# Attention scores from two rounded 4-byte parts in the two row halves of the array, in one ring of three double buffers

## What is computed

```python
x = x + layernorm(attention(layernorm(x)))      # 16 heads of size 8, rotary positions, causal softmax
x = x + layernorm(ffn(layernorm(x)))            # 16 experts, top 2, and 2 shared experts

q, k, v = split(h @ Wq + bq), split(h @ Wk + bk), split(h @ Wv + bv)
q, k = apply_rope(q, cos, sin), apply_rope(k, cos, sin)
att = einsum('bhqd,bhkd->bhqk', q, k) / sqrt(8)
att = softmax(where(causal, att, -1e10))
y = einsum('bhqk,bhkd->bhqd', att, v).reshape(B, T, 128) @ Wp + bp
```

## Time and profile before

| | |
|---|---|
| median of 3 runs | 1123.39 us (1121.81 to 1124.06) |
| the profiled execution | 1124.22 us |
| its span on the core | 1122.3 us |
| mean granted TensorE clock | 0.964 |
| PE busy | 1048.8 us (93%) |
| DVE busy | 835.8 us (74%) |
| POOL busy | 826.6 us (74%) |
| ACT busy | 745.5 us (66%) |

### The profile page before, as it was taken

The page is one execution under the profiler, slowest core; times in us unless marked ns, Lnnn a source line. Parts: engine busy times, 40 slices in busy tenths (PEclk is TensorE's granted clock), DMA queues, the critical chain, the costliest instruction groups (busy, mean ns, idle before and its releaser), DMA issues.

```text
span 1122.3 us, 26491 instructions
## 1 busy us (share of the span) xinstructions
PE 1048.8 (93%) x8228; PEld 668.9 (60%) x8228; DVE 835.8 (74%) x2265; ACT 745.5 (66%) x1619; POOL 826.6 (74%) x976
## 2 busy tenths in 40 slices
PE   3379999999999999999999999999977999999996
PEld 2255555656666566565665656656453787877742
DVE  5378888888788878888888887887255777777644
ACT  5117778787787877778777787787823666666434
POOL 6536678788888978888788886666844766666757
PEclk8559999999999999999999999999988999999998
DMA  6333333414243242432424323241556444554376
GB/s 95 110 105 119 93 94 113 116 63 121 87 139 113 63 120 73 148 109 74 122 64 140 111 79 112 73 127 38 133 156 106 137 136 137 154 155 134 109 250 199
DMA packets 109747, 129.88 MB, mean 116 GB/s; under 512 B 17723, under 2 KB 90412, under 8 KB 105004
## 3 DMA queue, kind: packets, MB, share of 16 engines
q1 hardware_dynamic: 100908, 110.04, 35.0%
q0 software_dynamic: 8704, 18.17, 4.8%
HBM read 80.99 MB, written 45.50 MB: 113 GB/s over the span
## 4 chain that ended last, share of the span: by engine, by line
PE 77%; DVE 9%; issue 2%; POOL 1%; DMA 1%; ACT 1%; SPq 0%; POOLq 0%; DVEq 0%; ACTq 0%
PE heads_ps L1535 13%; PE score L1525 10%; PE wide L1677 8%; DVE mx L1324 7%; PE wide L1499 6%; PE wide L1564 6%; PE score L1511 4%; PE wide L1566 4%; PE wide L1660 3%; PE wide L1661 3%; PE score L1651 3%; PE wide L1598 2%; PE misc L1543 2%; PE wide L1590 1%; PE wide L1618 1%
## 5 line engine op out<-in xcount | busy, mean ns | idle before, releaser
L978 ACT ACTIVATE values<-score 128x512 f32<-128x512 f32 (+1 forms) x704 | 369.0, 558 | 90.7 <-PE score L1525 81.0
L1324 DVE TENSOR_REDUCE mx<-wide 128x2 f32<-128x1024 f32 (+3 forms) x384 | 387.5, 1039 | 48.5 <-PE wide L1566 45.6
L1525 PE MATMUL score<-qk 75*128 75x512 bf16 (+3 forms) x1024 | 229.8, 301 | 1.7 <-ACT values L978 0.9
L890 POOL TENSOR_SCALAR_AFFINE_SELECT values<-values 128x512 f32<-128x512 f32 x256 | 162.1, 644 | 88.2 <-ACT values L978 87.9
L935 POOL DMA_INDIRECT token_scratch<-spread,e_id x144 | 137.9, 957 | 71.0 <-issue 52.9
L1564 PE MATMUL wide<-qk 72*128 72x384 bf16 (+2 forms) x768 | 168.3, 279 | 9.9 <-DVE mx L1324 4.9
L1535 PE MATMUL heads_ps<-values 128*32 128x512 f32 (+3 forms) x2048 | 174.3, 441 | 0.2 <-POOL values L890 0.2
L1566 PE MATMUL wide<-qk 118*128 118x128 bf16 x1024 | 170.8, 222 | 2.4 <-DVE mx L1324 1.5
L879 POOL DMA_INDIRECT sorted_scratch<-zr,places x128 | 134.0, 1047 | 48.9 <-issue 27.4
L1525 PEld LDWEIGHTS score<-qk 75*128 75x128 bf16 x1024 | 84.8, 98 | 89.8 <-ACT values L978 46.8
L1564 PEld LDWEIGHTS wide<-qk 72*128 72x128 bf16 x768 | 76.0, 99 | 65.5 <-DVE mx L1324 19.0
(11 more groups left out here) (192 smaller groups left out, 1991.3 us busy)
## 6 DMA issues: line engine op xcount, KB each, us to landing
qk<-parts_scratch SPq DMA_DIRECT2D x192, 192.0 KB
parts_scratch<-spread SPq DMA_DIRECT2D x16, 768.0 KB, 8.3
qk<-sorted_scratch SPq DMA_DIRECT2D x144, 66.5 KB
front<-token_scratch SPq DMA_DIRECT2D x16, 512.0 KB, 4.8
xt<-attn_x SPq DMA_DIRECT2D x16, 256.0 KB, 8.6
xr<-attn_x SPq DMA_DIRECT2D x16, 256.0 KB, 8.8
x_scratch<-z SPq DMA_DIRECT2D x16, 256.0 KB, 6.2
shared_scratch<-s_out SPq DMA_DIRECT2D x16, 256.0 KB, 8.8
```

The source lines that it names most:

```text
L890: nc.gpsimd.affine_select(out=prob[n][:, :, 0:P], in_=prob[n][:, :, 0:P], compare_op=ALU.is_ge, fill=0.0, base=0, pattern=[[0, HG], [1, P] ...
L978: nc.scalar.activation(free_ap(prob[kb][:, hs_[0], :], [[1, N * len(hs_)]]), score[SCORE_RING.buffer(b, step)][:, 0:N * len(hs_)], ACT.Exp ...
L1324: nc.vector.tensor_reduce(mx[:, h0:h0 + len(hs_), j:j + 1], src, axis=AX.X, op=ALU.max).then_inc(p1_max, 1)
L1525: last = nc.tensor.matmul(score[SCORE_RING.buffer(b, step)][:, k * N:(k + 1) * N], k4[e][0:SROWS, h, kb * P:(kb + 1) * P], q4[e][0:SROWS, ...
```

## The change

- **Parts.** Queries and keys are split into two parts of a rounded 4-byte type (`F32R`) in place of three bf16 parts: ACT writes the first, DVE the second; the steps `second` and `third` go. Four products of parts make 32 rows, with two maximum rows 34 (`SROWS`), with the staircase (five entries in a row) 60 (`MROWS`).
- **Row halves.** Head h lies in partitions 0 to 63 and head h + 8 in 64 to 127 of the same column block. Each matmul of p and s is issued once for each half, into the two banks of one buffer. The number of score matmuls of a batch stays: 64 in s, 112 in p.
- **Units.** s has 6 units for a group in place of 11; an exponential reads both banks. p keeps 24 units for a batch.
- **Ring.** One ring of three buffers of two banks for p, s, D and the rest (60 uses in a pass); the ring of `score` goes.
- **Heads.** The value blocks of even groups stand in columns 0 to 8, of odd groups in 9 to 17, and two groups accumulate in the same PSUM bank: two copies, two sets of four transposes and two reciprocals for a batch in place of four; the products on DVE stay four; the copy of V becomes two.
- **Maxima.** Two parts: step O and one ACT operation go; four DMAs for half the heads in place of three.
- **DMA.** Parts to DRAM 1024 KB for a batch (768 before); 20 shuffle transfers for a batch in place of 14.
- **Start.** The staircase is spread by two ACT copies and eight DMAs from the ACT queue, in place of two ACT and two DVE copies and two DMAs.
- **Order.** `START`, `ORDER` and `DRAIN` are new.

```diff
-P1_UNITS = [(3, (0, 1)), (3, (2, 3)), (2, (0, 1)), (2, (2, 3)), (1, (0, 1, 2, 3)), (0, (0, 1, 2, 3))]
-P2_UNITS = ([(0, (h,)) for h in range(HG)] + [(1, (h,)) for h in range(HG)]
-            + [(2, (0, 1)), (2, (2, 3))] + [(3, (0, 1, 2, 3))])
+P1_UNITS = [(3, (0,)), (3, (1,)), (2, (0,)), (2, (1,)), (1, (0, 1)), (0, (0, 1))]
+P2_UNITS = [(0, (0,)), (0, (1,)), (1, (0,)), (1, (1,)), (2, (0, 1)), (3, (0, 1))]
...
+    "v3.1@-1 mask2.1 p18@0 s0.0 rnormal v3.2@-1 p19@0 v3.3@-1 s0.1 p20@0 heads1@-1 s0.2 p21@0 s0.3 p22@0 K place Y "
+    "rstd s0.4 p23@0 v0.0 s0.5 cos s1.0 W p0 M1@0 mask2.2 N1@0 normal zstats s1.1 mask2.3 v0.1 s1.2 mask3.0 p1 U1 G1 "
+    "d3 v0.2 p2 s1.3 v0.3 p3 s1.4 H2 mask3.1 d4 p4 v1.0 p5 s1.5 p6 s2.0 p7 mask3.2 v1.1 s2.1 d5 p8 sin0@4 v1.2 "
+    "mask3.3 v1.3 H0@-1 d6 p9 mask0.0@1 s2.2 sin1@4 U2 d7 V rstats G2 mask0.1@1 sin2@4 p10 s2.3 sin3@4 stats d0@-1 "
+    "s2.4 d1@-1 mask0.2@1 heads0 mask0.3@1 p11 s2.5 d2@-1 T v2.0 s3.0 p12 v2.1 s3.1 mask1.0@1 zrstd@0 p13 rX v2.2 "
+    "mask1.1@1 M0 Z@0 p14 s3.2 rL choose N0 mask1.2@1 X@4 s3.3 p15 v2.3 mask1.3@1 residual@0 v3.0 chosen rexp s3.4 "
+    "p16 R@4 U0@-1 G0@-1 D mask2.0@1 Q@4 H1@-1 s3.5 rrstd@0 p17 "
...
-WIDE_STEPS = ("V", "X", "Q", "Y", "W", "T", "p", "rX", "rL", "U")
+WIDE_STEPS = ("V", "X", "Q", "Y", "W", "T", "p", "rX", "rL", "U", "s", "D", "rows")
-    WIDE_RING = Ring(B, lambda step: int(step.what in WIDE_STEPS), 2)
-    SCORE_RING = Ring(B, lambda step: SCORE_STEPS.get(step.what, 0), 2)
+    WIDE_RING = Ring(B, lambda step: int(step.what in WIDE_STEPS), 3)
...
+            for n in range(2):
+                nc.scalar.activation(qkr[0:HALF_ROWS, n, 0, :], free_ap(stairs[:, n, :], [[0, NT], [1, P]]), ACT.Copy).then_inc(stairs_set, 1)
+            act.wait_ge(stairs_set, 2)
+            for e in range(2):
+                for side in range(2):
+                    first = 0 if e or side else 1
+                    for n in range(2):
+                        act.dma_start(words[side * HALF_ROWS + ROWS:(side + 1) * HALF_ROWS, 2 * e + n, first:NH // 2, :],
+                                      free_ap(words[ROWS:HALF_ROWS, n, 0, :], [[0, NH // 2 - first], [1, T]])).then_inc(rows_filled, 16)
...
-                        for k, h4 in enumerate(hs_):
-                            h = g * HG + h4
-                            last = nc.tensor.matmul(score[SCORE_RING.buffer(b, step)][:, k * N:(k + 1) * N],
-                                                    k4[e][0:SROWS, h, kb * P:(kb + 1) * P], q4[e][0:SROWS, h, kb * P:T],
-                                                    start=True, stop=True)
+                        for k, c in enumerate(2 * g + m for m in of_):
+                            for side in range(2):
+                                rows = slice(side * HALF_ROWS, side * HALF_ROWS + SROWS)
+                                last = nc.tensor.matmul(unit[:, side, k * N:(k + 1) * N], k_r[e][rows, c, kb * P:(kb + 1) * P],
+                                                        q_r[e][rows, c, kb * P:T], start=True, stop=True)
...
-                                                    vext[e][:, n, g * HG + h4, :], prob[n][:, h4, :],
-                                                    start=(n == 0), stop=(n == NT - 1))
+                                                    vext[e][:, n, h4 // 2 * (NH // 2) + 2 * g + h4 % 2, :], prob[n][:, h4, :],
+                                                    start=(g % PAIR == 0 and n == 0), stop=(g % PAIR == PAIR - 1 and n == NT - 1))
```

More of the change, by code:

```diff
@@ L261, in program @@
         rot = view(front, F32, [NT, 2, P], 6 * NT * P)
-        spread = sb("spread", [P, 2 * T + NPART * T])
-        rest = view(spread, F32, [2, T])
-        parts = view(spread, BF16, [2, NPART, T], 2 * 2 * T)
-        qk4 = sb("qk4", [P, 4, NH, T], BF16)
-        q4 = [qk4[0:MROWS, 2 * n, :, :] for n in range(2)]
-        k4 = [qk4[0:MROWS, 2 * n + 1, :, :] for n in range(2)]
+        spread = sb("spread", [P, 2 * QPART * T])
+        parts = view(spread, F32, [2, QPART, T])
+        parts_r = view(spread, F32R, [2, QPART, T])
+        with nc.sbuf_tensor("qk_rounded", [P, 4, NH // 2, T], F32R) as qkr:
+            pass
+        qk4 = sb("qk4", [P, 4, NH // 2, T])
+        words = qkr[:].bitcast(F32)
+        q_r = [qkr[:, 2 * n, :, :] for n in range(2)]
+        k_r = [qkr[:, 2 * n + 1, :, :] for n in range(2)]
         VEXT = NT * NH * 32
@@ L376, in wide_free @@
                 eng.wait_ge(s_gate_biased, c * NCH + user.n + 1)
+            elif user.what == "s":
+                eng.wait_ge(exp_done, (c * NG + user.group) * P2_N + user.n + 1)
+            elif user.what == "rows":
+                eng.wait_ge(p_done, 3)
             else:
                 eng.wait_ge(read_by[user.what], c + 1)
[L380 to L384, removed]
-            user, c, _ = last
-            if user.what == "s":
-                eng.wait_ge(exp_done, (c * NG + user.group) * P2_N + user.n + 1)
-            else:
-                eng.wait_ge(s_out_ready, c + 1)
         def misc_free(eng, b, step):
@@ L616, in _, with rows_of @@
                           free_ap(blank[:], [[1, SPARE], [1, ROW]], SPARE)).then_inc(spare_filled, 16)
+            def rows_of(side, at, count):
+                return slice(side * HALF_ROWS + at, side * HALF_ROWS + at + count)
             def maxima_in(b, e, half):
                 sp.wait_ge(m_ready[half], b + 1)
-                for r in range(NPART):
-                    sp.dma_start(q4[e][ROWS + r:ROWS + r + 1, half * NH // 2:(half + 1) * NH // 2, :],
-                                 mparts[half][:, r, :]).then_inc(m_in[half], 16)
@@ L625, in shuffle @@
[L625 to L639 removed]
+                heads_ = slice(half * NH // 4, (half + 1) * NH // 4)
@@ L917, in body @@
                         nc.gpsimd.tensor_tensor(z[:], z[:], xr[:], ALU.add).then_inc(x1_ready, 1)
-                    elif step.what == "third":
-                        pool.wait_ge(part2_ready, b + 1)
-                        nc.gpsimd.tensor_tensor(parts[:, n, 2, :], rest[:, n, :], parts[:, n, 1, :],
-                                                ALU.subtract).then_inc(part3_ready, 1)
             pool.wait_ge(ident_ready, N_IDENT)
@@ L969, in body @@
                     if step.what in WIDE_STEPS:
-                        unit = wide[WIDE_RING.buffer(b, step)]
+                        unit = pairs[WIDE_RING.buffer(b, step)]
                     if step.what == "s":
-                        kb, hs_ = P2_UNITS[n]
+                        kb, of_ = P2_UNITS[n]
                         u = g * P2_N + n
@@ L1042, in body @@
                         wait(act, parts_out, 16 * b)
-                        nc.scalar.activation(parts[:, :, 0, :], unit[:], ACT.Copy).then_inc(part1_ready, 1)
-                    elif step.what == "stairs" and n % 2 == 1:
-                        nc.scalar.activation(free_ap(qk4[HALF_ROWS:P, n - 1, 0, :], [[P, NH * NT], [1, P]]),
-                                             free_ap(stairs[HALF_ROWS:P, 0, :], [[0, NH * NT], [1, P]]), ACT.Copy).then_inc(q_stairs, 1)
-                    elif step.what == "second":
-                        act.wait_ge(rest_ready, b + 1)
-                        nc.scalar.activation(parts[:, :, 1, :], rest[:], ACT.Copy).then_inc(part2_ready, 1)
+                        nc.scalar.activation(parts_r[:, :, 0, :], unit[:], ACT.Copy).then_inc(part1_ready, 1)
             iterations(act, body)
@@ L1100, in _ @@
             for n in range(2):
-                nc.vector.memset(vext[n][:, :, :, HS:HS + 1], 1.0).then_inc(filled, 1)
+                for k in range(PAIR):
+                    last = nc.vector.memset(free_ap(vext[n][:, 0, 0, :], [[4 * 32, NT * NH // 4], [32, 2], [1, 1]],
+                                                    k * (2 * 32 + WIDTH) + HS), 1.0)
+                last.then_inc(filled, 1)
             for rows in (bp_rows,):
```

229 lines of the change are left out of this document (111 added, 118 removed), and 20 rows, old and new, of tables (DRAIN, ORDER, START).

## The result

The changed kernel takes 1158.64 us (median of 4 runs, 1150.48 to 1165.41) where the kernel before takes 1123.62 in the same comparison: ratio 1.0312, interval 1.0236 to 1.0387, slower by 3.1%. I had forecast 5.4% faster; the time lies inside my range, but on the other side of the forecast and not for the reason that I gave to that side. The profiled execution took 1165.41 us, the longest of the four; their mean granted clocks are 0.922, 0.926, 0.938 and 0.945 for 1165.41, 1162.40, 1154.88 and 1150.48 us, so the trace shows more of the low clock than the median execution has.

The account below looks back on a forecast made before the run. TensorE's stream was taken as the bound: a pass of 47.5 us falls to 43.2, plus 0.3 for the ring, 43.5. With start and other passes 60 us go: 1063 us, 5.4% faster, range 1033 to 1172.

Parts of the forecast that it names:

- What bounds the kernel: In the loop: TensorE's stream is the bound, busy 47.3 of 47.5 us a pass, next engines 7 to 8 us behind.
- Score matmuls, 11.4 us: Steps s and p on TensorE: paired halves overlap, 128-column pairs bound by 4-byte loads; 11.4 us a pass replaces 17.9.
- Changes of height, 0.12 us each: TensorE switching between row halves and other modes: 26 more switches a pass at 0.12 us, 3.1 us added.
- The stream, 43.2 us: TensorE's sum for a pass: 47.5 - 17.9 - 0.9 + 11.4 + 3.1 = 43.2 us.
- The ring, 0.3 us: One ring of three buffers, 60 uses a pass, three quarters filled: 0.3 us added, giving a 43.5 us pass.
- rival 4: The one ring lets late VectorE maxima hold s too: pass 45.5 to 47.5 us, 1090 to 1122 us; chance 0.14.
- Start, -2 us: Before the passes: staircase copies go, eight transfers come; -2 us within -4 to +6, first score matmul after 55 refutes.
- The clock "should stay at 1.00 in the loop, since PE is still busy without a pause": TensorE's granted clock in the loop: stays at 1.00 because TensorE is busy without a pause.
- Rival 1: Every p and s pair: loads take turns (1177 us) or rounded columns take twice the time (1154 us); chance 0.23.
- Rivals 2 and 3: Score matmuls: four times the column time, some 1420 us, chance 0.06; no load bound, free switches, 1033 us, chance 0.13.

Follow-up runs that it names:

- e3: Kernel before with two groups of heads accumulated in one PSUM bank, the rest kept in bf16 with its order: 1126.76 us, ratio 1.0021.
- e6: Changed kernel with VectorE's maxima of step p over only the first 128 columns of each tile: 1140.65 us, pass at clock 1.00 46.0 us.
- e10: Changed kernel with score matmuls reading only the upper two bytes of each number: 1148.49 us (kernel before there 1198.73), steady pass 44.86 us.
- e4: Changed kernel with one tiny full-height 16-column matmul ahead of each of the 24 p steps: 1287.03 us, steady pass 54.55 us.
- e5: Changed kernel with one tiny half-height 16-column matmul ahead of each of the 24 p steps: 1197.64 us, steady pass 48.77 us.
- e9: Kernel before with every score matmul over the first 60 rows, still 2-byte: 1258.66 us (kernel before there 1198.73), steady pass 51.06 us.
- e7: Changed kernel with the router's logits biased in PSUM and read there by the subtraction: 1185.59 us (before 1125.23), steady pass 47.15 us.
- e1: Changed kernel plus 16 full-height 512-column matmuls ending the start and two ahead of each p step of pass 0: 1163.86 us, ratio 1.0335.
- e11: e7 plus two full-height 512-column matmuls before p18 to p23 and before every p of batches 0 and 1: 1241.68 us (kernel before there 1198.73).
- e2: Changed kernel with staircase rows written by VectorE and ScalarE copies instead of eight transfers: 1149.94 us, ratio 1.0241.
- e12: Changed kernel with the edits of e2 and e7 and the fills of e11, one instead of two in later passes: 1167.55 us, ratio 1.0387.

## Why the prediction was wrong

The spans differ from my forecast by 101 us: 47.5 in the ten steady passes, 34.5 in passes 0 and 1, 12 in the rest, 7 in the start. Three steps failed: the sum of 43.2 us for PE's stream, with the 0.3 us of the ring on top of it (46.0 us, and 2.05 us of waits), the clock that should stay at 1.00 (0.50 for 85 us of passes 0 and 1), and the start.

- **What bounds the kernel.** PE's stream, I wrote. It is nearly so, but not in the stretch ahead of step Y, where the chain runs through VectorE. There PE was idle for only 0.2 us in a pass of before, so the stretch hardly shows while PE is full, and it took the first 0.9 us that e3 took from PE: the pass stayed at 47.48 us and fell to 46.63 when VectorE was lightened.
- **Score matmuls, 11.4 us.** The column rate was right, the halves do run side by side, and 128-column pairs follow at 0.11 us: all three choices held. The term was still too small, since I let only the 128-column pairs be bound by their loads. The wider pairs pay too: 0.34 instead of 0.22 for 512, 0.22 instead of 0.11 for 256 (medians of a pass of e6). In one pass of e6 I added up the starts: the 176 score matmuls hold TensorE for 17.6 us, 8.5 in columns, 4.6 more between one pair and the next, 2.7 at changes to other steps, 1.7 at four waits. That is 13.1 for the pairs, 1.7 over my term; e10 puts the whole price of 4-byte operands at 3.5 us of busy time.
- **Changes of height, 0.12 us each.** Right in size: 0.05 to 0.1 by e4, e5 and e9.
- **The stream, 43.2 us.** 46.0 in e6: 1.7 from the wider pairs; 0.9 of idle PE behind ScalarE's exponentials and VectorE, and some 0.2 not placed.
- **The ring, 0.3 us.** Too small. From e6 to e7 1.15 us are VectorE's maxima, and another 0.9 the blocked subtraction: rival 4 in kind and, with a pass of 48.05, a little above its 47.5. The blocked subtraction is a meeting of GpSimd and VectorE that the new order made; in before it took 0.22 or 0.23 us in all 16 batches.
- **Start, -2 us.** +5.0; the first score matmul is at 59.69 us, past the 55 that I had named as the refutation. The eight transfers hold ScalarE's queue for 15.65 us; without them it is +1, within what a start moves by itself.
- **The clock "should stay at 1.00 in the loop, since PE is still busy without a pause".** This step failed and no rival held it; it makes 28 of the 41 us against before, and 34.5 of the 101 against the forecast. PE was busy without a pause from 100.00 to 138.72 us at 0.50. Ahead of the two falls the clock was at 1.00 and PE busy for 4.82 of 6.70 us (87.5 to 94.2) and for 6.15 of 6.60 us (142.1 to 148.7). Busy is not the same as working at full height and rate: the pairs use half of the rows for each product and wait for loads. Full-height fills hold the clock but for one dip (e1, e11), 2-byte operands leave 24 us of low clock in the first passes and none in the ten after them (e10), and half height in 2-byte type lets it fall in some passes (e9). So both the width of the operands and the height have a part; no run has 4-byte operands at full height, and their shares aren't told apart. The Trainium skill ("TensorE: Matmul & The Clock Gate", section Part 1: The HAM clock gate) ties the clock to how busy TensorE has been; by the engine's busy record the trace doesn't agree: at 0.50 TensorE is busy for 38.72 of 38.72 us. Why it rose at 125 us in e2 and at 186 in after, and why it falls in some of several equal passes, isn't settled.
- **Rivals.** Rival 1 ended near the result (1154 us) but its mechanism is refuted: neither loads in turn nor double columns. Rivals 2 and 3 are refuted by the same rows. That the time lies in my range, whose upper part was there for rival 1, is luck. So is part of its place: the four executions differ by 1.3%, where I had counted on 0.2%, and their order is that of their granted clocks.

## What to carry to other kernels

A change that makes a tuned TensorE stream lighter (fewer rows, wider operands with slower loads) can lose by the clock more than it saves in columns: compare the granted clock in the same stretches before the engine times, and price a stretch in which such work stands close together at both levels. When 4-byte operands are taken, charge the load to every pair, the wide ones too: here 0.11 in place of 0.06 us over 128 columns, and 0.11 or 0.12 us more over 256 to 512. And a wait just behind the bounding engine takes the first gain for itself: look in the chain of waits for each stretch of another engine, however short its visit.

## What the runs showed of the hardware that I had not expected

- TensorE at 100% busy with the granted clock at 0.50 for 39 us, and passes of the same kernel that differ by 7.35 us (47.15 and 54.5) by one such stretch of 17 us, with the same work ahead of it.
- Two full-height matmuls before each of six p steps held it in nine of ten steady passes (e11), one before each in eight of ten (e12).
- A 64-column VectorE subtraction of 0.22 us that takes 2.39 us beside two GpSimd instructions, and 0.22 again once one input lies in PSUM (e7) or once it comes 0.5 us earlier (e6).
- Eight transfers of 448 to 512 KB issued from ScalarE's queue that take 15.65 us to issue.
